# Unread matmul streams between the Householder columns of an eigensolver kernel, and Euler units spread over three quarters of them

## What is computed

```python
def euler_step(h, _):                       # block 0: 8 steps, adj is 512 x 512
    ax = jnp.einsum('nm,bmd->bnd', adj_mx, h)
    f = alph * 0.5 * (ax - h) + h @ w_eff - h + x0
    return (h + dt * f, None)
...
L_norm = d_inv_sqrt[:, None] * L * d_inv_sqrt[None, :]      # block 1
_, U = jnp.linalg.eigh(L_norm)
agg = jnp.einsum('mn,bnd->bmd', U.T, features)
h = jax.nn.relu(agg @ W1 + b1)
out = h @ W2 + b2
return jnp.einsum('nm,bmd->bnd', U, out)
```

## Time and profile before

| what | us |
|---|---|
| median of 3 runs | 5474.12 |
| the profiled execution | 5465.82 |
| its span, first to last instruction | 5463.9 |
| VectorE busy | 4301.3 (79%) |
| TensorE busy | 2558.9 (47%) |
| first column to last column | about 3000 |

### The profile page before, as it was taken

How to read it: one execution, slowest core, us unless ns; L and a number is a source line. 1 busy time by engine, 2 the same in 40 slices (tenths; PEclk the granted TensorE clock), 3 DMA queues, 4 the chain that set the end, 5 groups by cost and what they waited for, 6 DMA issues and landing times.

```text
span 5463.9 us, 61609 instructions
## 1 busy us (share of the span) xinstructions
PE 2558.9 (47%) x10553; PEld 1941.6 (36%) x10553; DVE 4301.3 (79%) x24022; ACT 1004.0 (18%) x4375; POOL 938.2 (17%) x4428
## 2 busy tenths in 40 slices
PE   6888888888767666666666100000000010200377
PEld 5656565656555544445666100000000000100243
DVE  7778878777788877777777888888788889899524
ACT  2232322333333333332222100000000000000000
POOL 2321111222222222223333111111000000000000
PEclk9678777877755555555555555555555555555688
DMA  1000000000000000000000000000000000000001
GB/s 43 1 1 1 1 1 1 1 1 1 1 1 1 1 1 1 1 1 1 1 1 1 26 0 0 0 0 0 1 0 0 0 0 0 0 0 0 0 0 31
DMA packets 16070, 16.97 MB, mean 3 GB/s; under 512 B 3056, under 2 KB 12400, under 8 KB 15472
## 3 DMA queue, kind: packets, MB, share of 16 engines
q1 hardware_dynamic: 15216, 13.47, 0.8%
q10 hardware_dynamic: 512, 0.02, 0.0%
HBM read 9.25 MB, written 4.19 MB: 2 GB/s over the span
## 4 chain that ended last, share of the span: by engine, by line
DVE 55%; PE 32%; issue 7%; ACT 3%; POOL 3%; DVEq 1%; ACTq 0%; DMA 0%; POOLq 0%; another core or an unknown queue 0%
PE ps L699 7%; DVE h L2067 5%; PE ps L688 5%; PE ps L744 4%; PE ps L646 2%; PE ps L638 2%; PE ps L624 2%; DVE ps L1396 2%; DVE small L1410 2%; DVE am L1309 1%; DVE hT L1694 1%; DVE small L1394 1%; DVE h L2069 1%; DVE am L1429 1%; DVE small L1390 1%
## 5 line engine op out<-in xcount | busy, mean ns | idle before, releaser
L699 PEld LDWEIGHTS ps<-UR 128*128 128x128 f32 x2552 | 498.2, 275 | 277.0 <-issue 95.5
L699 PE MATMUL ps<-UR 128*128 128x41 f32 (+17 forms) x2552 | 515.3, 341 | 125.0 <-ACT UR L1169 68.9
L744 PE MATMUL ps<-small,ones 128*128 128x2 f32 x766 | 198.8, 329 | 504.6 <-DVE am L1429 504.4
L744 PEld LDWEIGHTS ps<-small,ones 128*128 128x128 f32 x766 | 167.8, 272 | 662.0 <-DVE am L1429 654.4
L822 PE MATMUL ps<-ident,m 128*128 128x128 f32 x36 | 9.0, 427 | 823.0 <-DVE small L2167 823.0
L766 PE MATMUL ps<-ones,qs 32*1 32x1 f32 x16 | 1.5, 158 | 821.2 <-DVE qs L1802 821.2
L969 POOL TENSOR_SCALAR small<-small 128x1 f32<-128x1 f32 x511 | 117.4, 230 | 1528.9 <-ACT small L1138 1512.4
L680 PE MATMUL ps<-UR,ident 128*128 128x18 f32 (+2 forms) x1020 | 288.5, 369 | 89.8 <-DVE UR L1398 89.8
L688 PE MATMUL ps<-ident,UR 128*128 128x128 f32 x1148 | 307.0, 399 | 28.1 <-DVE UR L1298 4.9
L822 PEld LDWEIGHTS ps<-ident,m 128*128 128x128 f32 x36 | 7.0, 222 | 825.0 <-DVE small L2167 825.0
L2067 DVE RECIPROCAL h<-h 128x512 f32<-128x512 f32 (+2 forms) x50 | 295.7, 5913 | 1.7
(11 more groups left out here) (693 smaller groups left out, 8777.7 us busy)
## 6 DMA issues: line engine op xcount, KB each, us to landing
out<-xs SPq DMA_DIRECT2D x4, 1024.0 KB, 4.5
m<-in_adj SPq DMA_DIRECT2D x1, 1024.0 KB, 5.2
before<-c_before SPq DMA_DIRECT2D x1, 1024.0 KB, 5.8
notafter<-c_notafter SPq DMA_DIRECT2D x1, 1024.0 KB, 7.6
sib<-c_sib SPq DMA_DIRECT2D x1, 448.0 KB, 8.5
eye<-c_eye SPq DMA_DIRECT2D x1, 256.0 KB, 2.5
iota<-c_iota SPq DMA_DIRECT2D x1, 256.0 KB, 2.9
leafsel<-c_leaf SPq DMA_DIRECT2D x1, 256.0 KB, 3.0
```

What stands on the lines that cost most here:

```text
L699: last = nc.tensor.matmul(ps[2][:, 0:2 * npend + 3], over(x_of(j)), flat[:, j, 2 * first:2 * k + 3], start=(j == tp), stop=(j == T - 1))
L744: nc.tensor.matmul(ps[3][:, 8:10], ones[:, :], CY, start=True, stop=True).then_inc(cy_ready, 1)
```

## The change

The number of Euler units per column falls from three to two: places 0 and 2 in the first two quarters, places 1 and 2 in the third, until all 551 are done. Beside them stand new matmuls that nothing reads. Each multiplies W1s with W2s, which are loaded at the start, into PSUM bank ps[1]. `keep_clock(halves)` issues that many of 256 columns; `keep_clock_narrow` issues some of 128 columns in the last quarter, 1, 1, 1 and 3 at four places of a column. The scalar sums that stood in ps[1] move to columns 64 and 65 of bank ps[4]. Before the loop TensorE waits until the weights are loaded.

In the first 8 columns there are no units, but 2, 8 and 2 streams at the three places for two columns and 2, 3 and 2 for six. After them place 1 has 3 streams where n_on = 4 (1 where there is panel work), 2 where n_on = 3 (0 with panel work), and 1 where n_on = 2 (0 with panel work). Once the units are used up, each unit that is wanted is replaced by two streams.

```diff
+EULER_UNITS = 551
+NARROW_STREAMS = (1, 1, 1, 3)
...
+        units_of, halves_of = [], []
+        for k in range(N - 1):
+            n_on, panel = window_of(k)[1], panel_stage(k)
+            matmuls = bool(panel) and panel[1] < 2 + panel[4]
+            wanted = (1, 0, 1) if n_on > 2 else (0, 1, 1) if n_on == 2 else (0, 0, 0)
+            extra = (0, 1 if matmuls else 3, 0) if n_on == 4 else (0, 0 if matmuls else 2, 0) if n_on == 3 else                 (0, 0 if matmuls else 1, 0) if n_on == 2 else (0, 0, 0)
+            if k < 2:
+                extra = (2, 8, 2)
+            elif k < 8:
+                extra = (2, 3, 2)
+            units = wanted
+            if k < 8:
+                units = (0, 0, 0)
+            left = EULER_UNITS - sum(sum(u) for u in units_of)
+            if k >= 8 and left < sum(wanted):
+                units, extra = (0, left, 0), (2 * wanted[0], 2 * wanted[1] + extra[1] - 2 * left, 2 * wanted[2])
+                extra = tuple(max(0, e) for e in extra)
+            units_of.append(units)
+            halves_of.append(extra)
...
         def euler_units(k):
 
-            return (0, 0, 0) if k < 8 or window_of(k)[1] < 3 else (0, 4, 1) if k < 10 else (1, 1, 1)
+            return units_of[k]
...
-                    nc.tensor.matmul(ps[1][:, 0:1], ones[:, :], SPART, start=True, stop=True).then_inc(s_ready, 1)
+                    nc.tensor.matmul(ps[4][:, 64:65], ones[:, :], SPART, start=True, stop=True).then_inc(s_ready, 1)
...
+            def keep_clock(halves):
+
+                for _ in range(halves):
+                    nc.tensor.matmul(ps[1][:, 0:2 * P].rearrange("p (a d) -> p a d", a=2), W1s[:, :],
+                                     W2s[:, :].unsqueeze(1).broadcast_to([P, 2, D]), start=True, stop=True)
+
+            def keep_clock_narrow(k, place):
+
+                if window_of(k)[1] == 1:
+                    for _ in range(NARROW_STREAMS[place]):
+                        nc.tensor.matmul(ps[1][:, 0:P], W1s[:, :], W2s[:, :], start=True, stop=True)
+
+            pe.wait_ge(weights_loaded, 16 * 8)
...
                 for _ in range(euler_units(k)[0]):
                     next(state, None)
+                if n_on > 1:
+                    keep_clock(halves_of[k][0])
...
+                    keep_clock_narrow(k, 0)
                     if k > narrow_from:
                         reflected_product(k - 1)
+                    keep_clock_narrow(k, 1)
                     pivot_row()
+                    keep_clock_narrow(k, 2)
                 for _ in range(euler_units(k)[1]):
                     next(state, None)
+                if n_on > 1:
+                    keep_clock(halves_of[k][1])
...
                 for _ in range(euler_units(k)[2]):
                     next(state, None)
+                keep_clock(halves_of[k][2])
+                keep_clock_narrow(k, 3)
...
-                    has_hk = h_.mark(ts(HK, ps[1][:, 0:1], RQ, -0.5, ALU.mult, ALU.mult))
+                    has_hk = h_.mark(ts(HK, ps[4][:, 64:65], RQ, -0.5, ALU.mult, ALU.mult))
```

More of the change, by code:

```diff
@@ L658, in reflected_product @@
                     pe.wait_ge(z_ready, k + 1)
-                    nc.tensor.matmul(ps[1][:, 0:1], ones[:, :], SPART, start=True, stop=True).then_inc(s_ready, 1)
+                    nc.tensor.matmul(ps[4][:, 64:65], ones[:, :], SPART, start=True, stop=True).then_inc(s_ready, 1)
                 else:
                     pe.wait_ge(zq_ready, k + 1)
-                    nc.tensor.matmul(ps[1][:, 0:2], z[:, 0:1].broadcast_to([P, P]), flat[:, tp, 2 * k:2 * k + 4:3],
+                    nc.tensor.matmul(ps[4][:, 64:66], z[:, 0:1].broadcast_to([P, P]), flat[:, tp, 2 * k:2 * k + 4:3],
                                      start=True, stop=True).then_inc(s_ready, 1)
+            def keep_clock(halves):
[7 more added lines that the diff above has]
+            pe.wait_ge(weights_loaded, 16 * 8)
             state = euler()
@@ L1393, in householder @@
                     dve.wait_ge(s_ready, k)
-                    has_hk = h_.mark(ts(HK, ps[1][:, 0:1], RQ, -0.5, ALU.mult, ALU.mult))
+                    has_hk = h_.mark(ts(HK, ps[4][:, 64:65], RQ, -0.5, ALU.mult, ALU.mult))
                     h_.wait(has_hk)
                     has_fix = h_.mark(stt(out=ps[2][:, 2 * npend - 1:2 * npend], in0=NA[:, 0:1], scalar=HK,
-                                          in1=NA[:, 1:2] if nb > 1 else ps[1][:, 1:2], op0=ALU.mult, op1=ALU.add))
+                                          in1=NA[:, 1:2] if nb > 1 else ps[4][:, 65:66], op0=ALU.mult, op1=ALU.add))
                     stt(out=column_of(k - 1, slice(tb, T), 1), in0=column_of(k - 1, slice(tb, T), 0), scalar=HK,
```

## The result

The changed kernel takes 5591.06 us (median of 4 runs) against 5471.41 us before (4 runs): a ratio of 1.0215, 95% interval 1.0186 to 1.0243. The forecast was 5310 with a range of 5110 to 5480, so it had the wrong sign and missed the range. The changed kernel is slower by 2.1%.

What follows compares the result with a forecast made beforehand. The prediction took TensorE's granted clock, full or half, to decide what a column costs. Quarter terms -135, -15, -18 and +6 sum to -162 from the 5463.9 us span, giving 5302, stated as 5310, range 5110 to 5480.

Steps and rivals of the forecast that it cites:

- The prices at full clock: Time per column at full clock, by quarter: 6.1, 5.5, 4.72 and 3.5 us.
- The stream's length: On TensorE, a stream of 256 columns takes 0.44 us at full and 0.85 at half; one of 128, 0.22 and 0.43.
- The parts set at nothing: Moved sums, weight wait, instruction fetch and fewer dependent units together zero; the first 8 columns were separately put at 60 us.
- The third quarter: 129 columns, 4.72 us at full and 6.83 at half, share 0.7: 5.20 us a column, 671 us, -18.
- my formula: In each quarter, a column costs 1 / (s / full + (1 - s) / half), from its two clock prices.
- the shares s: Part of each quarter at full clock: 0.75, 0.65, 0.7 and 0.6, first to fourth.
- Fourth quarter, s = 0.6: 128 columns, 3.5 us at full and 4.93 at half: 3.96 us a column, 507 us, +6.
- the last quarter never leaves half: Sign that the forecast is wrong: the last quarter stays at half clock, with columns of 4.9 us.
- the stuck case: Rival: last quarter drops to half clock and stays, 4.93 us a column, +131 there, 5437 in all; chance 0.17.
- the slower case: Rival: streams at half clock make TensorE's passes the ring; third +59, last +131, second +34, first -119: 5579; chance 0.10.
- Second quarter, s = 0.65: 128 columns, 5.5 us at full and 8.3 at half: 6.24 us a column, 798 us against 813.2, -15.
- First quarter: 119 columns at 6.74 us, 802 us, plus 60 for the first 8 columns: 862 against 997.0, -135.

Runs made afterwards that it cites:

- the last run: No streams in the first 8 columns, against the kernel with eight streams a column in the last quarter and 12 in a row: 5157.15 us in one run.
- e6: Against e4, place 1 gets two streams instead of three in every second-quarter column, panel columns included: 5292.98 us, ratio 0.9666.
- e4: Against the changed kernel without last-quarter streams, place 1 filled in every column (3, 3 and 1 streams by quarter): 5214.52 us, ratio 0.9533.

## Why the prediction was wrong

What held:
- **The prices at full clock.** 6.12 us a column in the first quarter (forecast 6.1), 4.69 in the third (4.72), 3.49 in the last (3.5). The first and the third are stretches of the changed kernel, as is the last quarter at half clock, 5.12 (4.93). The first quarter's stretch at half, 10.2 against 9.8, isn't like for like: its three columns have panel work and one stream, and the forecast was for three streams.

```profile
571.90:608.60 36.70, 1.03 (x6) 1.00 0.01 1
2010.10:2103.80 93.70, 3.42 (x20) 1.00 0.01 1
291.10:321.70 30.60, 0.51 (x3) 0.50 0.00 1
2512.50:2563.70 51.20, 1.71 (x10) 0.50 0.00 1
```

- **The stream's length.** 1.42 us for three of 128 columns at half (0.43 each and a tail), as taken from the rows and not half of it. The page TensorE: Matmul & The Clock Gate of the Trainium skill (Back-to-back issue gap) gives N / 1.2, 107 ns for 128 columns at half. Counted for each pass, as the prediction did, the last quarter's three streams would take 0.64 us, and counted for each call 0.32. The trace disagrees, by a factor of two for a pass: 1.42 us with the tail, six passes of 0.213.
- **The parts set at nothing.** The sums in ps[4] cost nothing (500.20 us for the last quarter without its streams, against 500.43 before), the start of the loop came 2 us later, and the first 8 columns cost 59.6 against the 60 taken.
- **The third quarter** went better than forecast: -56 and not -18, at a share of 0.84 and not 0.7. With 0.84 my formula gives 1 / (0.84 / 4.72 + 0.16 / 6.83) = 4.97 us, 636 us for 128 columns; measured 633.

What failed is the shares s, the part of a quarter's time at full clock, which I chose and couldn't take from a row:
- **Fourth quarter, s = 0.6.** It was 0, but for the first column, and "the last quarter never leaves half" is one of the signs by which the forecast was to be called wrong. This one term is 157 (+163 where I had +6) of the 277 us between the forecast span of 5302 and the 5579.3 of the profile. I priced the stuck case rightly in kind (+131) and gave it 0.17, plus its part in the slower case. What I hadn't weighed is that a state that can be lost and not regained has no middle share: 0.6 is the mean of two outcomes, and neither of them is near it. The runs show the cost (163 us, gone when the streams are), that with six streams the quarter never gets back to full clock once it is at half, with or without the rest of the change, and that full clock once given held, in the one run of it, for some 27 columns only. What drops it at the turn stays open: the changed kernel has a bare stretch there, but the last run passes the same stretch at 1.00 with eight streams behind it, and no run changed the turn alone.
- **Second quarter, s = 0.65.** It was 0.52, and the cost was +76 against -15. I wrote that panel columns are barer than today, and that two streams are as much as a unit of 512, and then kept today's share. The runs with panel columns and place 1 filled (e6 and e4) show that both count: 59 us for the bare panel columns, 73 for the third stream. Together that is 132 us, and the quarter then beats the -15 forecast by 45 (753 against 813.2 - 15 = 798).
- **The formula itself** is too kind where the clock flips often. With the measured share of 0.52 it gives 1 / (0.52 / 5.5 + 0.48 / 8.3) = 6.56 us, 840 for the quarter; measured 889. In the first, with its 0.62, it gives 7.12 us, 848; measured 868. It fits where the clock rarely moves (third quarter). Either a fall is paid in the stretch where TensorE is fullest, or the prices are too low: the stretch of 6.12 us has no panel call in it, and with place 1 filled the formula gives the first quarter 1 / (0.82 / 6.1 + 0.18 / 9.8) = 6.54 us, 779, where it took 818. No run separates the two.
- **Second quarter's price at full clock, 5.5.** As a mean over the quarter it is likely a little low: with three units and one stream the quarter stood at 0.97 and still took 748.27 / 128 = 5.85 us a column, though that is another mix. With 5.8 in place of 5.5 the formula gives 868 for the quarter of the changed kernel, so a good half of the formula's miss can be this price.
- **First quarter**: -69 and not -135, at a share of 0.62 and not 0.75; 20 us of it are the formula's. The panel columns once more: filling them took the quarter from 925 us to between 874 and 893 in four kernels that have it so.
- **The slower rival** came out at 5579, and the result is 5591. That isn't a hit of its terms: it had the third quarter at +59 (it was -56) and the last at +131 (it was +163). Its mechanism, streams at half clock as the ring, is the one that decided, in the last quarter alone.
- **Two smaller figures of the prediction** don't come out of its own numbers. A tenth of share is worth 32 to 35 us in the first quarter by the formula and 16 to 32 in the others, not up to 50. Half of the way from 5020 to the forecast is 5165 and not 5130. Neither changes the outcome.

## What to carry to other kernels

Filler that is there to hold the clock has two prices, and the one at half clock decides whether to add it: work that is hidden at full clock is the critical path at half. Ask of each stage whether it regains full clock by itself once it has lost it; if not, its expected time isn't a mean of the two, and either enough filler for that (here eight streams and not six) or none is right. Look for the barest kind of column first: streams in the panel columns alone took the kernel without the last quarter's streams from 5411 to 5293 us.

## What the runs showed of the hardware

- In the last quarter the streams' number flips the outcome: six of them in a column gave 5.12 us and a clock of 0.50 in all but the first of 127 columns, eight gave 3.5 us at 0.99. Two more streams are worth 207 us with the 12 in a row (663.29 against 455.86) and 192 without (471.37).
- TensorE can be busy 655.62 of 663.29 us and stay at 0.50 (below, all engines, the last quarter of the changed kernel), while it holds 1.00 at 80.11 busy of 93.70 us in the third, with streams of 256 columns. So the busy share in the profile doesn't tell which level is granted.

```profile
2476.20:3139.49 663.29, 655.62 (x2833) 611.56 (x2833) 380.68 (x2802) 119.53 (x525) 189.49 (x1016) 0.50 0.00 1
2010.10:2103.80 93.70, 80.11 (x442) 61.40 (x442) 83.64 (x603) 37.92 (x184) 29.84 (x160) 1.00 0.01 1
```
